# A vision block on one Trainium2 core: the base rows of an image are written one step later in the attention pipeline

## The chip, the cores and the metric

One core of one Trainium2 chip runs the whole kernel. The metric is the device time of one execution in microseconds (us); the figure for a kernel is the median of its runs. The kernel is written engine by engine: TensorE (PE in the profile, its weight loads PEld), VectorE (DVE), ScalarE (ACT), GpSimd (POOL) and SyncE (SP, which issues most DMAs) each run their own in-order program, and semaphores join them.

## The reference

32 images of 256 x 256 go through three stages.

```python
# 1. three-level Haar transform, bands weighted by softmax/sigmoid gates, transformed back
h = _L0_tok_ref(x, Wa, ba, Wd1, bd1, Wd2, bd2, Wd3, bd3)
h = jnp.concatenate([broadcast(cls_tok), h], axis=1)          # 257 tokens of 256
# 2. causal attention of layernorm(h) with itself
e = _layernorm(h)
scores = einsum('bnd,bmd->bnm', einsum('bnd,de->bne', e, R), e) + mask
h = h + einsum('bnm,bmd->bnd', softmax(scores), e)
# 3. eight experts, each takes the k tokens it scores highest
h = h + _L0_ffn_ref(_layernorm(h), gate_w, gamma, beta, fc1s, b1s, fc2s, b2s)
```

The expert stage starts from `xf`, the layernormed rows, and adds the experts' weighted outputs to them, so the result is `h1 + layernorm(h1) + experts`. The attention stage therefore writes two things for every image: the "base rows" `h1 + layernorm(h1)` straight to the output (the scatter of the experts adds to them later), and the "expert rows", the twice-normalised input that the experts gather.

## The kernel before, in words

**Stages.** The images are loaded and their gate logits computed (to about 55 us of the span); then a software pipeline takes the 32 images through transform and attention (55 to 337 us); then 26 bisection rounds find the experts' thresholds (337 to some 400 us); then the experts run to the end.

**The pipeline.** It has 36 steps, one per new image, and 4 more to drain. In step t five images are in flight: image t (called `a`, and `nxt` is t+1), `b` = t-1, `c` = t-2, `d` = t-3 and `m` = t-4. `LAG` is 4. `steps()` (line 259) emits for each engine first `HEAD` steps written out, then a hardware loop (`Fori`, line 267) of four steps per pass (`UNROLL`) up to `TAIL` = 28, then steps 28 to 35 written out. With `HEAD` = 4 the loop makes six passes, steps 4 to 27. An `emit` function per engine fixes that engine's order within a step. In step t:

- TensorE: the inverse transform of `b` into bank `Hb` (L778), four transposes of `c` into `Tb` (L786), the forward transform of `a` (L793), three transposes of the exponentials of `d` (L801), keys of `c` times R (L809), the attention product of `d` (L816 to L818), the scores of `c` into `Sb` (L826, L828).
- VectorE: statistics of `b` from `Hb` (L1140, L1146), the row-sum reciprocal (L1152), band weights and inverse columns of `a` (L1159 to L1177), `U` of `d` from the attention product (L1183), **the update `H1` of `d`** (L1191, two instructions), then gate scores (L1198) and **the negated row maxima of `c`** (L1202), and statistics of `H1` (L1208, L1214).
- GpSimd: waits for the statistics, takes them to the power -0.5 (L475), makes the scales and biases; L480 is the last of them and signals `nrm`. Then it makes the forward columns of image t+1 (L440 to L447; L447 signals `xc`) and stores the statistics (L483).
- ScalarE: **exponentials** of `d` (L598, L600), the copy of the transposed encoding `ET` (L605), the copy of the transposed exponentials `PTS` (L610), **the copy of the inverse** `hc` (L614), the copy of the keys `GT` (L617), the layernormed rows `Ex` of `b` (L624, needs `nrm`), the expert rows `Yp` of `m` (L632) and **the base rows `Bs` of `m`** (L638, two instructions).
- SyncE: stores the base rows of `m` after semaphore `base`, then the expert rows after `yp`.

Two lines tie the base rows to others. Both buffers of `H1` are reused every second image, so VectorE waits before L1191:

```python
after(dve, "base", d.n - 1)        # in step t: base rows of image t-5 are written
```

The exponentials of the next step wait for `nmax` of L1202. `N6`, `O1`, `ST` hold biases, plus-one scales and scales of a step in two buffers by the step's parity.

Of the kernel before, what the change touches and what calls it, by code (L numbers as in the profile page):

```python
# [6 lines left out]
ACT = mybir.ActivationFunctionType  # L7
# [8 lines left out]
NB = 32  # L16
NH = 2
# [30 lines left out]
def build_program(nc, x, cls_tok, Wa, ba, Wd1, bd1, Wd2, bd2, Wd3, bd3, R, gate_w, gate_wT, gamma, beta,  # L48
                  fc1T, b1, fc2T, b2, b2T, const, out, debug=None):
    ctx = ExitStack()  # L50
    with ctx:
        def sb(name, shape, dt=F32):
            return ctx.enter_context(nc.sbuf_tensor(name, shape, dt))

        def sem(name):
            return ctx.enter_context(nc.semaphore(name))
# [121 lines left out]
        H1 = [sb(f"H1{i}", [P, NH, D]) for i in range(2)]  # L178
        Bs = [sb(f"Bs{i}", [P, NH, D]) for i in range(2)]
# [7 lines left out]
        N6 = [sb(f"N6{i}", [P, 6]) for i in range(2)]  # L187
        O1 = [sb(f"O1{i}", [P, 2]) for i in range(2)]
# [43 lines left out]
        s = {n: sem(n) for n in names}  # L232

        def after(eng, name, count):

            if not isinstance(count, int) or count > 0:
                eng.wait_ge(s[name], count)
# [6 lines left out]
        LAG = 4  # L244
# [6 lines left out]
        class Step:  # L251

            def __init__(self, i, k):
                self.n, self.p, self.r = i * UNROLL + k, k % 2, k % 4
                self.h = i * (UNROLL // 2) + k // 2

        HEAD, TAIL = 4, 28

        def steps(eng, emit):


            def images(i, k, bounded):
                return [Step(i, k)] + [Step(i, k + d) if not bounded or 0 <= k + d < NB else None
                                       for d in range(1, -LAG - 1, -1)]
            for k in range(HEAD):
                emit(*images(0, k, True))
            with eng.Fori(HEAD // UNROLL, TAIL // UNROLL) as i:
                for k in range(UNROLL):
                    emit(*images(i, k, False))
            for k in range(TAIL, NB + LAG):  # L270
                emit(*images(0, k, True))
# [295 lines left out]
        def _(act):  # L567
# [5 lines left out]
            A = nc.scalar  # L573
            for h in range(NH):
                for n, levels in enumerate(((1, 3), (2,))):
                    act.wait_ge(s["rep"], 2 * h + n + 1)
                    for lv in levels:
                        last = A.activation(bsum[h][lv], RB[h][lv][1], ACT.Copy)
# [6 lines left out]
            A.activation(z2[:, 1:NJ], z2[:, 1:NJ], ACT.Exp)  # L585
            A.activation(z2[:, 0:1], zz[:, 0:1], ACT.Exp, scale=-1.0).then_inc(s["z_e"], 1)

            def emit(t, _nxt, _a, b, c, d, m):
                if isinstance(t.n, int) and t.n == EARLY + 7:
                    act.wait_ge(s["gt_c"], 6)  # L590
                    A.activation(GM[:, 0:EARLY, :, :], GL[:, 0:EARLY, :, :], ACT.Tanh).then_inc(s["gt_t"], 1)
                if d:

                    after(act, "pt", d.n - 1)
                    after(act, "u", d.n - 1)
                    after(act, "rv", d.n - 1)
                    act.wait_ge(s["nmax"], d.n + 1)
                    A.activation(Pr[d.p][:, 0:129], Sb[:, KEYS[0][0]:KEYS[0][1]], ACT.Exp, bias=nmx[d.p][:, 0:1],  # L598
                                 accum_out=rsm[d.p][:, 0:1])
                    A.activation(Pr[d.p][:, 129:386], Sb[:, KEYS[1][0]:KEYS[1][1]], ACT.Exp, bias=nmx[d.p][:, 1:2],  # L600
                                 accum_out=rsm[d.p][:, 1:2]).then_inc(s["pexp"], 1)
                if c:
                    after(act, "sm", c.n - 1)
                    act.wait_ge(s["et"], c.n + 1)
                    A.activation(ET[c.p][:, :, 1:NT], Tb[:, :].rearrange("p (c t) -> p c t", c=2), ACT.Copy)\  # L605
                        .then_inc(s["et_ev"], 1)
                if d:
                    after(act, "av", d.n - 1)
                    act.wait_ge(s["pt"], d.n + 1)
                    A.activation(PTS[d.p][:, :], Pb[:, 0:384], ACT.Copy).then_inc(s["pt_ev"], 1)  # L610
                if b:
                    after(act, "h1", b.n - 3)
                    act.wait_ge(s["st0_b"], b.n + 1)
                    A.activation(hc[b.r][:, :, :], Hb[:, :].rearrange("p (h c) -> p h c", h=NH), ACT.Copy)  # L614
                if c:
                    act.wait_ge(s["er"], c.n + 1)
                    A.activation(GT[c.p][:, :, NE + 1:], Rb[:, :].rearrange("p (c t) -> p c t", c=2), ACT.Copy)\  # L617
                        .then_inc(s["er_ev"], 1)
                if b:

                    after(act, "av", b.n - 3)
                    act.wait_ge(s["nrm"], t.n + 1)
                    for h in range(NH):
                        last = A.activation(Ex[b.r][:, h, 0:D], Hb[:, h * D:(h + 1) * D], ACT.Identity,  # L624
                                            bias=N6[t.p][:, h:h + 1], scale=ST[t.p][:, 8 + h:9 + h])
                    last.then_inc(s["hcE"], 1)
                if m:

                    after(act, f"yp_st{m.p}", m.h * 16)
                    act.wait_ge(s["nrm"], t.n + 1)  # L630
                    for h in range(NH):
                        last = A.activation(Yp[m.p][:, h, :], H1[m.p][:, h, :], ACT.Identity,  # L632
                                            bias=N6[t.p][:, 4 + h:5 + h], scale=ST[t.p][:, 12 + h:13 + h])
                    last.then_inc(s["yp"], 1)

                    after(act, f"base_st{m.p}", m.h * 16)
                    for h in range(NH):
                        last = A.activation(Bs[m.p][:, h, :], H1[m.p][:, h, :], ACT.Identity,  # L638
                                            bias=N6[t.p][:, 2 + h:3 + h], scale=O1[t.p][:, h:h + 1])
                    last.then_inc(s["base"], 1)  # L640
            steps(act, emit)

            def high(eh, q, layer, half):

                hi = (w1s, w2s)[layer][eh][0]
                act.wait_ge(s["wld"], (q * 2 + layer + 1) * 16)
                A.activation(flat(hi, half), raw[:, half * NF:(half + 1) * NF], ACT.Copy).then_inc(s["whi"], 1)  # L647
# [56 lines left out]
            act.wait_ge(s["ld_par"], 112)  # L704
            high_rows(Job(0, 0))
            jobs(act, emit)


# [811 lines left out]
```

## Time and profile before

| | us |
|---|---|
| median of 3 runs | 878.05 (875.82 to 880.17) |
| the profiled execution's own time | 877.11 |
| its span on the engines | 875.2 |
| the attention pipeline, 36 steps | 282 of it |
| busy share of the span: PE / PEld / DVE | 85% / 72% / 66% |
| busy share of the span: ACT / POOL | 52% / 53% |

The busy shares are averages over stages of different kinds. In the pipeline four engines work in turn on each image, and each is idle part of every step; what sets the pace there is read from who waits for whom.

### The profile page before, as it was taken

To read this page: it belongs to the slowest core of one execution; us is meant where nothing else is said; L and a number is where in the kernel's file an instruction comes from. 1 tells how busy PE (TensorE), PEld (TensorE's weight loads), DVE (VectorE), ACT (ScalarE), POOL (GpSimd) and SP (SyncE) were. 2 spreads that over 40 slices of the span, in tenths; PEclk is the share of its full clock that TensorE was granted. 3 is DMA by queue.
4 is the path that set the end of the run, shared out by engine and by line. 5 is a ranking of instruction groups with operands and counts; after the bars stand their busy time and mean duration, and the time that the engine had idled before them with its cause. 6 is when DMAs were issued, how large, how long until landed. Compare 5 with 4: busy or idle time off the path is not lost.

```text
span 875.2 us, 15546 instructions
## 1 busy us (share of the span) xinstructions
PE 743.0 (85%) x4349; PEld 627.9 (72%) x4349; DVE 580.8 (66%) x1951; ACT 452.6 (52%) x998; POOL 463.5 (53%) x744
## 2 busy tenths in 40 slices
PE   6977999999999972333799897998979989989994
PEld 3644666766676652222698897998979979889994
DVE  3835888888888866988776574574656836544341
ACT  1003677777777763000553765545646655366552
POOL 0127667776777743203336556565475664654723
PEclk9988999999999995555899999998999999989997
DMA  9400121122112226201123233334243342323312
GB/s 347 184 3 1 49 73 54 66 72 72 59 61 72 73 73 108 102 1 44 61 38 95 72 52 87 86 51 128 38 98 79 49 133 43 96 69 51 50 19 31
DMA packets 45448, 64.32 MB, mean 73 GB/s; under 512 B 13840, under 2 KB 40528, under 8 KB 42704
## 3 DMA queue, kind: packets, MB, share of 16 engines
q1 hardware_dynamic: 32400, 46.54, 15.9%
q0 software_dynamic: 12800, 17.12, 12.0%
q8 instruction: 24, 0.39, 0.2%
q14 instruction: 32, 0.26, 0.1%
q10 hardware_dynamic: 192, 0.00, 0.0%
HBM read 38.12 MB, written 25.53 MB: 73 GB/s over the span
## 4 chain that ended last, share of the span: by engine, by line
PE 32%; DVE 8%; issue 8%; POOL 7%; DMA 4%; ACT 3%; POOLq 1%; ACTq 0%; DVEq 0%; SPq 0%
PE bank L885 15%; PE bank L899 12%; DMA raw<-in_fc1T 3%; DVE ge L1242 2%; POOL w2l L494 2%; POOL yg L509 2%; POOL out L531 2%; DVE Tc L1258 1%; PE bank L874 1%; ACT bank L668 1%; PE bank L922 1%; PE bank L864 1%; PE bank L911 1%; DMA yg<-rows,idx 1%; ACT hh L671 1%
## 5 line engine op out<-in xcount | busy, mean ns | idle before, releaser
L1365 DVE TENSOR_TENSOR hl<-bank,hh 128x384 fp32r<-128x384 f32 (+1 forms) x192 | 97.5, 513 | 167.7 <-ACT hh L671 165.4
L531 POOL DMA_INDIRECT out<-ob,sidx x72 | 113.9, 1582 | 165.4 <-ACT ob L684 153.8
L668 ACT ACTIVATE bank<-bank,b1s 128x384 f32<-128x384 f32 (+1 forms) x192 | 99.5, 518 | 134.4 <-PE bank L885 133.9
L885 PE MATMUL bank<-yh,w1h 128*128 128x384 f32 (+1 forms) x384 | 137.8, 359 | 27.4 <-DVE hl L1365 26.1
L885 PE MATMUL bank<-yh,w1l 128*128 128x384 f32 (+1 forms) x384 | 127.5, 332 | 0.0
L885 PE MATMUL bank<-yl,w1h 128*128 128x384 f32 (+1 forms) x384 | 127.4, 332 | 0.0
L899 PE MATMUL bank<-w2l,hh 128*128 128x256 f32 x384 | 108.0, 281 | 0.0
L899 PE MATMUL bank<-w2h,hh 128*128 128x256 f32 x384 | 108.0, 281 | 0.0
L899 PE MATMUL bank<-w2h,hl 128*128 128x256 f32 x384 | 107.9, 281 | 0.0
L509 POOL DMA_INDIRECT yg<-rows,idx x72 | 72.4, 1006 | 62.9 <-issue 57.8
L885 PEld LDWEIGHTS bank<-yh,w1h 128*128 128x128 f32 x384 | 77.3, 201 | 32.7 <-DVE hl L1365 28.7
L671 ACT ACTIVATE hh<-bank 128x384 fp32r<-128x384 f32 (+1 forms) x192 | 87.8, 457 | 6.1
L885 PEld LDWEIGHTS bank<-yl,w1h 128*128 128x128 f32 x384 | 77.0, 200 | 0.0
L885 PEld LDWEIGHTS bank<-yh,w1l 128*128 128x128 f32 x384 | 76.2, 198 | 0.0
L899 PEld LDWEIGHTS bank<-w2l,hh 128*128 128x128 f32 x384 | 72.6, 189 | 0.0
L899 PEld LDWEIGHTS bank<-w2h,hl 128*128 128x128 f32 x384 | 72.5, 189 | 0.0
L899 PEld LDWEIGHTS bank<-w2h,hh 128*128 128x128 f32 x384 | 72.5, 189 | 0.0
L809 PE MATMUL bank<-ET,Rw 128*128 128x256 f32 x256 | 62.9, 388 | 0.0
L494 POOL TENSOR_TENSOR w1l<-raw,w1h 128x1024 fp32r<-128x1024 f32 x16 | 37.8, 2368 | 34.7 <-ACT w1h L647 34.6
L809 PEld LDWEIGHTS bank<-ET,Rw 128*128 128x128 f32 x256 | 45.9, 189 | 11.0 <-issue 5.2
L826 PE MATMUL bank<-GT,ET 128*128 128x137 f32 (+1 forms) x256 | 52.5, 340 | 0.7 <-ACT GT L617 0.7
L475 POOL TENSOR_TENSOR ST<-A,mhalf 128x6 f32<-128x6 f32 x36 | 50.0, 1389 | 3.0
(223 smaller groups left out, 1760.9 us busy)
## 6 DMA issues: line engine op xcount, KB each, us to landing
BIG<-in_x SPq DMA_DIRECT2D x4, 2048.0 KB, 18.9
out<-Bs SPq DMA_DIRECT2D x32, 256.0 KB, 2.2
rows<-Yp SPq DMA_DIRECT2D x32, 256.0 KB, 2.4
raw<-in_fc1T SPq DMA_DIRECT2D x8, 1024.0 KB, 4.8
raw<-in_fc2T SPq DMA_DIRECT2D x8, 1024.0 KB, 4.8
yg<-rows,idx POOLq DMA_INDIRECT x72, 2.9
out<-ob,sidx POOLq DMA_INDIRECT x72, 3.8
gwb<-in_gate_w SPq DMA_DIRECT2D x1, 1024.0 KB, 12.4
```

Of the source, the lines that this page charges most:

```text
L475: g.tensor_tensor(st[:, 8:14], A6[:, :], mhalf[:, :], ALU.pow).then_inc(s["pow"], 1)
L494: rest = g.tensor_tensor(flat(lo, half), raw[:, half * NF:(half + 1) * NF], flat(hi, half), ALU.subtract)
L509: g.indirect_dma_start(out=yg[eh][0:m, t, :], out_offset=None, in_=rows, in_offset=tok(ap=idx[eh][0:m, t:t + 1], axis=0))\
L531: g.indirect_dma_start(out=out_rows, out_offset=tok(ap=sidx[job.eh][0:m, t:t + 1], axis=0), in_=ob[t % 3][0:m, :], in_offset=None, compute ...
L668: A.activation(h[:, 0:cur.w], h[:, 0:cur.w], ACT.Gelu_apprx_tanh, bias=b1s[:, bass.ds(cur.e, 1), f]).then_inc(s["hact"], 1)
L671: A.activation(hT[cur.p][0][:, f, 0:cur.w], h[:, 0:cur.w], ACT.Copy).then_inc(s["hhi"], 1)
L809: last = T.matmul(Rb[:, e * D:(e + 1) * D], Rw[:, j, e * P:(e + 1) * P], ET[c.p][:, j, 1:NT], start=(j == 0), stop=(j == 1))
L826: T.matmul(Sb[:, c0:c0 + w], ET[c.p][:, j, 1 + h * P:1 + (h + 1) * P], GT[c.p][:, j, 0:w], start=(j == 0), stop=False)
L885: last = T.matmul(Lb[ring(cur, f)][:, 0:cur.w], w1s[cur.eh][i][:, d, f * P:(f + 1) * P], yT[cur.p][k][:, d, 0:cur.w], start=(n == 0), stop ...
L899: mm = T.matmul(bank[4 + t % 2][:, 0:D], hT[prev.p][i][:, f, at:at + P], w2s[prev.eh][k][:, f, :], start=(n == 0), stop=(n == 23))
L1242: last = v.tensor_scalar(ge[:, eh, :], V[:, eh, :], tried[:, eh:eh + 1], None, ALU.is_ge, ALU.add, accum_out=cnt[:, eh:eh + 1])
L1365: v.tensor_tensor(hT[cur.p][1][:, f, 0:cur.w], Lb[ring(cur, f)][:, 0:cur.w], hT[cur.p][0][:, f, 0:cur.w], ALU.subtract).then_inc(s["hlo"], 1)
```

## The change

ScalarE's base rows leave the end of step t. A function `base_rows` writes them in step t+1, after the copy of the inverse and ahead of the copy of the keys. In step t it is thus image t-5 whose base rows are written; biases and scales are those of step t-1, found by the image's own parity (the same buffers). The last image's base rows follow after the steps. So that the image five back has a valid index in the first pass of the loop, `HEAD` goes from 4 to 8: on every engine steps 4 to 7 are written out, and the loop makes five passes, steps 8 to 27.

```diff
             def __init__(self, i, k):
                 self.n, self.p, self.r = i * UNROLL + k, k % 2, k % 4
                 self.h = i * (UNROLL // 2) + k // 2
-
-        HEAD, TAIL = 4, 28
+                self.i, self.k = i, k
+
+            def back(self, d):
+
+                return Step(self.i, self.k - d)
+
+        HEAD, TAIL = 8, 28
...
+            def base_rows(m):
+
+                after(act, f"base_st{m.p}", m.h * 16)
+                for h in range(NH):
+                    last = A.activation(Bs[m.p][:, h, :], H1[m.p][:, h, :], ACT.Identity,
+                                        bias=N6[m.p][:, 2 + h:3 + h], scale=O1[m.p][:, h:h + 1])
+                last.then_inc(s["base"], 1)
+
...
                     A.activation(hc[b.r][:, :, :], Hb[:, :].rearrange("p (h c) -> p h c", h=NH), ACT.Copy)
+
+                if not isinstance(t.n, int) or t.n > LAG:
+                    base_rows(t.back(LAG + 1))
                 if c:
                     act.wait_ge(s["er"], c.n + 1)
...
                     last.then_inc(s["yp"], 1)

-                    after(act, f"base_st{m.p}", m.h * 16)
-                    for h in range(NH):
-                        last = A.activation(Bs[m.p][:, h, :], H1[m.p][:, h, :], ACT.Identity,
-                                            bias=N6[t.p][:, 2 + h:3 + h], scale=O1[t.p][:, h:h + 1])
-                    last.then_inc(s["base"], 1)
             steps(act, emit)
+            base_rows(Step(0, NB - 1))
```

ScalarE, one step inside the loop of the kernel before, up to the exponentials of the next step (`Pr` and `Ex` lie in the tile ARENA; L598 and L600 are the exponentials, L632 the expert rows, L638 the base rows):

```order
L614 ACTIVATE hc<-bank 128x512 [waits st0_b,h1]
L617 ACTIVATE GT<-bank 128x2x256 [waits er]
L622 REGISTER_ALU [waits av]
L624 ACTIVATE ARENA<-bank,N,ST 128x256 [waits nrm]
L624 ACTIVATE ARENA<-bank,N,ST 128x256
L632 ACTIVATE Yp<-H,N,ST 128x256 [waits nrm,yp_st1]
L632 ACTIVATE Yp<-H,N,ST 128x256
L638 ACTIVATE Bs<-H,N,O 128x256 [waits base_st1]
L638 ACTIVATE Bs<-H,N,O 128x256
L598 ACTIVATE ARENA,rsm<-bank,nmx 128x129 [waits rv,nmax,u,pt]
```

The same stretch of the changed kernel, where L611 is the first exponential and L597 the base rows:

```order
L627 ACTIVATE hc<-bank 128x512 [waits st0_b,h1]
L597 ACTIVATE Bs<-H,N,O 128x256 [waits base_st0]
L597 ACTIVATE Bs<-H,N,O 128x256
L633 ACTIVATE GT<-bank 128x2x256 [waits er]
L638 REGISTER_ALU [waits av]
L640 ACTIVATE ARENA<-bank,N,ST 128x256 [waits nrm]
L640 ACTIVATE ARENA<-bank,N,ST 128x256
L648 ACTIVATE Yp<-H,N,ST 128x256 [waits nrm,yp_st1]
L648 ACTIVATE Yp<-H,N,ST 128x256
L611 ACTIVATE ARENA,rsm<-bank,nmx 128x129 [waits rv,nmax,u,pt]
```

The two base-row instructions have gone from in front of the exponentials to the place between `hc` and `GT`.

VectorE, the end of step 3 and the begin of step 4, before: the loop is entered there.

```order
L1214 BN_AGGR ST<-bn 128x2 [waits st1_b]
L1214 BN_AGGR ST<-bn 128x2
L267 UNCONDITIONAL_BRANCH
L267 ISA
L1140 BN_STATS bn<-bank 128x6 [waits h0,tab]
L1140 BN_STATS bn<-bank 128x6
L1146 BN_AGGR ST<-bn 128x2 [waits st0_b]
L1146 BN_AGGR ST<-bn 128x2
L1150 REGISTER_ALU
```

The same place in the changed kernel:

```order
L1226 BN_AGGR ST<-bn 128x2 [waits st1_b]
L1226 BN_AGGR ST<-bn 128x2
L1152 BN_STATS bn<-bank 128x6 [waits h0,tab]
L1152 BN_STATS bn<-bank 128x6
L1158 BN_AGGR ST<-bn 128x2 [waits st0_b]
L1158 BN_AGGR ST<-bn 128x2
L1164 RECIPROCAL ST<-rsm 128x2 [waits tab,pexp]
```

Branch and register instructions are gone from steps 4 to 7; the loop is entered four steps later.

## Rows read from the trace of the kernel before

**Rows 1.** Busy time by engine in one pass of the loop; columns as named in its first line.

```profile
core 0: us, PE busy (x) PEld busy (x) DVE busy (x) ACT busy (x) POOL busy (x), PEclk, DMA share, GB/s
125.00:156.70 31.70, 31.15 (x142) 21.59 (x142) 27.42 (x97) 23.50 (x56) 22.89 (x66) 1.00 0.20 66
```

**Rows 2.** Timeline of ScalarE: start, length, engine, line, operation, idle time before.

```profile
126.18 1.08 ACT L632 ACTIVATE Yp<-H,N,ST 128x256 f32<-128x256 f32 x2
127.16 1.08 ACT L638 ACTIVATE Bs<-H,N,O 128x256 f32<-128x256 f32 x2
128.15 0.36 ACT L598 ACTIVATE ARENA<-bank,nmx 128x129 f32<-128x129 f32 x1
...
130.19 0.59 ACT L614 ACTIVATE hc<-bank 128x512 f32<-128x512 f32 x1
131.68 0.60 ACT L617 ACTIVATE GT<-bank 128x512 f32<-128x512 f32 x1 [0.90 <-PE bank L809]
...
135.93 0.37 ACT L598 ACTIVATE ARENA<-bank,nmx 128x129 f32<-128x129 f32 x1
```

**Rows 3.** Timeline of VectorE, steps 8 to 10: update and maxima.

```profile
125.77 1.42 DVE L1191 SCALAR_TENSOR_TENSOR H<-ARENA,ST,hc 128x256 f32<-128x256 f32 x2
...
127.20 0.61 DVE L1202 TENSOR_REDUCE nmx<-bank 128x1 f32<-128x129 f32 x2
...
133.02 0.89 DVE L1183 SCALAR_TENSOR_TENSOR ARENA<-CX,ARENA,bank 128x264 f32<-128x264 f32 x2 [0.68 <-PE bank L818]
134.00 1.20 DVE L1191 SCALAR_TENSOR_TENSOR H<-ARENA,ST,hc 128x256 f32<-128x256 f32 x2
...
135.21 0.61 DVE L1202 TENSOR_REDUCE nmx<-bank 128x1 f32<-128x129 f32 x2
...
141.80 1.04 DVE L1191 SCALAR_TENSOR_TENSOR H<-ARENA,ST,hc 128x256 f32<-128x256 f32 x2
...
142.85 0.61 DVE L1202 TENSOR_REDUCE nmx<-bank 128x1 f32<-128x129 f32 x2
```

**Rows 4.** Timeline of GpSimd, steps 8 to 10: last scale and the columns.

```profile
124.99 0.24 POOL L480 TENSOR_SCALAR O<-ST 128x2 f32<-128x2 f32 x1
...
127.66 0.29 POOL L447 TENSOR_TENSOR ARENA<-ARENA 128x64 f32<-128x64 f32 x1
...
132.64 0.24 POOL L480 TENSOR_SCALAR O<-ST 128x2 f32<-128x2 f32 x1
...
133.98 0.40 POOL L443 TENSOR_TENSOR ARENA<-ARENA 128x128 f32<-128x128 f32 x1
...
140.63 0.24 POOL L480 TENSOR_SCALAR O<-ST 128x2 f32<-128x2 f32 x1
```

**Rows 5.** Timeline of TensorE, step 9: forward transform, transposes, scores.

```profile
128.00 1.13 PE L793 MATMUL bank<-ARENA,C 128*128 128x512 f32 x2
129.19 0.52 PE L801 MATMUL bank<-C,ARENA 128*128 128x128 f32 x3
...
132.82 0.63 PE L826 MATMUL bank<-GT,ET 128*128 128x137 f32 x4
```

**Rows 6.** Timeline of VectorE, first instruction of a later pass of the loop.

```profile
152.70 0.76 DVE L1140 BATCH_NORM_STATS2 bn<-bank 128x6 f32<-128x256 f32 x2 [0.41 <-issue]
```

**Rows 7.** DMA issues of the page: size, us from issue to landing.

```profile
out<-Bs SPq DMA_DIRECT2D x32, 256.0 KB, 2.2
rows<-Yp SPq DMA_DIRECT2D x32, 256.0 KB, 2.4
```

**Rows 8.** Timelines of VectorE and GpSimd in the written-out steps 28 and 29.

```profile
285.35 0.61 DVE L1202 TENSOR_REDUCE nmx<-bank 128x1 f32<-128x129 f32 x2
...
291.00 0.24 POOL L480 TENSOR_SCALAR O<-ST 128x2 f32<-128x2 f32 x1
```

**Rows 9.** Timelines of ScalarE and VectorE, end of step 31 and step 32.

```profile
308.12 1.08 ACT L632 ACTIVATE Yp<-H,N,ST 128x256 f32<-128x256 f32 x2
...
310.09 0.35 ACT L598 ACTIVATE ARENA<-bank,nmx 128x129 f32<-128x129 f32 x1
...
308.82 0.62 DVE L1202 TENSOR_REDUCE nmx<-bank 128x1 f32<-128x129 f32 x2
```

## The prediction

> **What bounds the kernel now.** I read the busy time by stretch first. One pass of the loop, four images, takes 31.7 us, in which TensorE is busy for 31.15, VectorE 27.42, ScalarE 23.50, GpSimd 22.89 [rows 1]. ScalarE has time to spare, so moving its work can pay only through what it holds up. TensorE looks full, but the ends of its matmuls are modelled, so I read waits instead, engine by engine, in the timelines of steps 8 to 10.
>
> On ScalarE base rows run from 127.16 to 128.24, and the exponentials of step 9 start at 128.15, in their wake [rows 2]. The maxima they need were complete at 127.20 + 0.61 = 127.81 [rows 3]. The exponentials were late by 0.34. In step 10 they start at 135.93, and the maxima ended at 135.82: 0.11. The pattern repeats with the loop; summed over the four steps of a pass the lag is 0.34 + 0.12 + 0.34 + 0.33 = 1.13.
>
> A second chain passes ScalarE by. GpSimd's last scale ends at 125.23, 132.88 and 140.87 in steps 8 to 10 [rows 4]; the maxima end at 127.81, 135.82 and 143.46 [rows 3]. From maxima to the next step's last scale it is 132.88 - 127.81 = 5.07 and 140.87 - 135.82 = 5.05. From last scale to maxima it is 2.58, 2.94 and 2.59. Two of three are alike although the update L1191 began 0.54, 1.12 and 0.93 after the scale and lasted 1.42, 1.20 and 1.04. In steps 8 and 10 it ends at 127.19 and 142.84, both times 1.96 or 1.97 after the scale. So a later start is made good by a shorter run: the update is held by GpSimd's column instructions, which run right behind the scale. Starting the update earlier brings nothing there. In step 9 alone it began 0.02 after L443 had started (134.00 against 133.98) and ended 0.36 later than that rule. I take this as the central reading: **in three of four steps the pace comes from VectorE's statistics, GpSimd's scale and the column instructions, and a later exponential costs nothing there.**
>
> **The change, part by part.**
>
> *Base rows ahead of the exponentials, removed.* Expert rows end at 127.26, before the maxima [rows 2, 3], so the exponentials are bound by the maxima and start about 0.04 after them: 0.30 earlier in three steps of four, 0.08 in the fourth, 0.99 per pass.
>
> How much of that reaches the update? The transposes of the exponentials begin at 129.19, 1.04 after them, but TensorE first runs the forward transform, 128.00 to 129.13, which waits for GpSimd's last column at 127.95 [rows 4, 5]. Its end is modelled; between 0.06 (if the end is right) and 0.30 (if it drains early) is to be had. I take 0.2, because its two matmuls show 1.13 together while other groups on TensorE start some 0.1 before a modelled end.
>
> For step 9 the update then starts at about 133.8, some 0.18 before L443, as in step 10, where it starts 0.93 after the scale. It should go ahead of L443, end 1.96 after the scale, and the maxima come at 132.88 + 2.58 = 135.46 instead of 135.82: 0.36 gained. In the other three steps the scale itself follows the maxima before it by an unchanged 5.07, so nothing is gained. Steps of this kind are 5, 9, 13, 17, 21 and 25: 6 x 0.36 = **2.2 us**. Bounds: 0 (the update still loses the turn) and 7 passes x 0.99 = 6.9 (every lead kept).
>
> The Trainium skill, page "SBUF — State Buffer", section "Who interferes with whom", states that a VectorE instruction with two SBUF inputs and a GpSimd one that reads SBUF shut each other out, and that whichever starts first holds the port for its whole length. By that rule a lead of 0.06 would already do for step 9, and the sum would be the same 2.2 with either reading of TensorE; without it the smaller lead gives 0. The updates of steps 8 and 10 [rows 3, 4] agree with the exclusion; no row here has the update start so shortly before a column instruction.
>
> *Base rows between the copy of the inverse and the keys, added.* They take 1.08 together, and 0.98 until the next instruction can start [rows 2]. The gap there is from 130.19 + 0.5 to 131.68, 0.99: ScalarE idles 0.90 of it for TensorE's keys. It fits with nothing over. If it overruns, the scores at 132.82 [rows 5] stand 0.54 behind the end of the keys' copy (132.28), so up to about 0.4 more is covered as well. Cost 0; bounds 0 and, past the cover, 1 to 1 per step. The copy of the inverse keeps its place, and so does `Ex`, which waits for the scale.
>
> *Added wait.* The update of step t now waits for base rows written in the same step. They end about 3.6 after its exponentials; the update starts 5.85 after them (128.15 to 134.00). 2.2 us to spare, cost 0. Were it late, gate scores, maxima and statistics would queue behind it on VectorE.
>
> *The stores.* SyncE issues the base rows' store, then the expert rows' behind it, so both go out about 4 us later than their data now allow. They land in 2.2 and 2.4 us [rows 7], some 7 after the exponentials of that step, and the buffer of the expert rows is written again 5.7 into the next step, that is 13 or 14 after. Cost 0. The last image's base rows follow its expert rows directly, as before, long before the experts gather.
>
> *Steps 4 to 7 written out.* A pass of the loop costs VectorE 0.41 at its first instruction [rows 6]; one such place, at step 8, becomes an entry like that of step 4: at most 0.4 gained. On the other side, in the written-out steps 28 and 29 the scale ends 291.24 - 285.96 = 5.28 after the maxima [rows 8], against 5.07 in the loop: 0.2 lost in about two steps. Together 0; bounds -0.4 and +0.4.
>
> *The end.* From step 31 on GpSimd makes no columns. There expert rows end at 309.20, maxima at 309.44, and the exponentials start at 310.09 [rows 9]. Free of base rows they start 0.04 after maxima that come 0.2 sooner: 309.3, 0.8 gained; step 33 follows its maxima by 0.1 less. The rest drains in series, so **0.9 us** stays; bounds 0.5 and 1.0.
>
> Sum: 2.2 + 0.9 + 0 = 3.1 us. The experts' stage is untouched. The profiled execution took 877.11, 0.94 under the median of 878.05: 874.0 on its terms, 875.0 as a median.
>
> **The rivals.** A difference of 0.5%, 4.4 us, is about what a measurement of this kernel can tell from no change.
>
> *Nothing in the loop.* If the 0.06 is right, the update of step 9 starts at 133.94, 0.04 ahead of L443's recorded start. Whether that is early enough to get the turn no row says. If not, only the end is gained: 878.05 - 0.9 = 877.2. For it: the end of L793 as recorded. Against: matmul ends are modelled.
>
> *Every lead is kept.* If the 1.96 is a coincidence of steps 8 and 10 and the update really follows TensorE (VectorE waits 0.68 for it in step 9), each pass loses 0.99: 6.9 + 0.9 = 7.8, 870.2. For it: that wait, in three steps of four. Against: the sum 1.96 in two different phases, and step 8's update, which took 1.42 where the fastest take less than 1.05.
>
> *Slower: the keys are late.* ScalarE's gap before the keys is exactly filled. If base rows there wait for their store's semaphore, or the copy of the inverse starts later than now, the keys slip, then the scores, then TensorE's next inverse. It decides once the keys start more than 0.4 after their present 3.53 behind the exponentials; a slip of 0.65 would cost 0.25 in each of 28 steps, 7.0 us, of which the end gives back 0.9: 884.2. For it: TensorE shows only 31.70 - 31.15 = 0.55 idle per pass, so it cannot absorb more. Against: the store's buffer was released a step earlier, and nothing ahead of the copy moves back.
>
> **How the numbers follow.** The forecast, a gain of 2 to 4.4 us: 0.52. Nothing in the loop, gain of 0 to 2: 0.21. Every lead kept, or most, over 4.4: 0.20. Slower by over 4.4: 0.07. Faster by over 0.5% is 0.20 and, since single runs before lay between 875.82 and 880.17, 0.07 of the forecast whose median may fall past the bound: 0.27. Slower 0.07; the same is what is left of the forecast, 0.45, and the 0.21: 0.66. The range leaves out the upper end of the slower case and what lies beyond every lead kept: 870.0 to 879.5. The forecast's own range is 873.5 to 876.5.
>
> **What would show it.** Exponentials starting 0.04 behind the maxima in every step; base rows in the gap ahead of the keys, whose start stays 3.5 behind the exponentials; maxima still 2.58 after the last scale, now in step 9 too; a pass of about 31.3 instead of 31.7. It is wrong if a pass is 30.7 or less (the leads are kept), stays 31.7 (the turn is lost), or if the keys move past 3.9.

## The result, and the profile after

The changed kernel takes 873.84 us (median of 18 runs, 870.72 to 876.80) against 877.66 for the kernel before (18 runs, 875.75 to 880.17): ratio 0.9954, 95% interval 0.9942 to 0.9967, a gain of 3.8 us. The forecast was a gain of 3.1. Its profiled execution took 872.07.

The page of the changed kernel, its span and busy times by engine:

```profile
span 870.1 us, 15450 instructions
PE 738.9 (85%) x4349; PEld 627.7 (72%) x4349; DVE 581.5 (67%) x1951; ACT 452.4 (52%) x998; POOL 464.7 (53%) x744
```

Each engine runs as many instructions as before; the 96 that are gone from the total (15546 before) are sequencer instructions. The line numbers move: L611 is the first exponential (L598 before), L597 the base rows (L638), L648 the expert rows (L632), L633 the keys' copy (L617), L1203 the update (L1191), L1214 the maxima (L1202), L485 the last scale (L480), L445 and L446 the two wide column instructions (L440, L441), L448 the first narrow one (L443), L805 the forward transform (L793), L813 the transposes (L801).

To keep out what varies from execution to execution in the rest of the kernel, I measure the pipeline from the end of the maxima of step 3 to the end of those of step 33. The maxima of these two steps on VectorE, in the kernel before:

```profile
87.48 0.60 DVE L1202 TENSOR_REDUCE nmx<-bank 128x1 f32<-128x129 f32 x2
...
324.31 0.61 DVE L1202 TENSOR_REDUCE nmx<-bank 128x1 f32<-128x129 f32 x2
```

and in the changed one:

```profile
88.12 0.61 DVE L1214 TENSOR_REDUCE nmx<-bank 128x1 f32<-128x129 f32 x2
...
321.23 0.61 DVE L1214 TENSOR_REDUCE nmx<-bank 128x1 f32<-128x129 f32 x2
```

That is 236.84 before and 233.12 after: 3.72 us, nearly the whole 3.8 of the medians. A second trace of the changed kernel gives 233.12 again. (The spans differ by 5.1. The rest goes with the execution: the maxima of step 3 came 0.64 later, the last steps took 1.4 less, see the end of this document, and the stages behind 0.6 less.)

ScalarE of the changed kernel, from the expert rows of step 12 to the keys' copy of step 13:

```profile
158.13 1.08 ACT L648 ACTIVATE Yp<-H,N,ST 128x256 f32<-128x256 f32 x2
159.52 0.37 ACT L611 ACTIVATE ARENA<-bank,nmx 128x129 f32<-128x129 f32 x1 [0.31 <-DVE nmx L1214]
161.89 0.59 ACT L627 ACTIVATE hc<-bank 128x512 f32<-128x512 f32 x1
162.37 1.09 ACT L597 ACTIVATE Bs<-H,N,O 128x256 f32<-128x256 f32 x2
163.35 0.60 ACT L633 ACTIVATE GT<-bank 128x512 f32<-128x512 f32 x1
```

The exponentials now wait for the maxima, where they had come in the wake of the base rows [rows 2]; the base rows lie in the gap ahead of the keys. So the change does what it says. VectorE of the changed kernel, update and maxima of step 9, then of steps 12 and 13:

```profile
134.10 1.29 DVE L1203 SCALAR_TENSOR_TENSOR H<-ARENA,ST,hc 128x256 f32<-128x256 f32 x2
135.40 0.61 DVE L1214 TENSOR_REDUCE nmx<-bank 128x1 f32<-128x129 f32 x2
...
157.47 1.32 DVE L1203 SCALAR_TENSOR_TENSOR H<-ARENA,ST,hc 128x256 f32<-128x256 f32 x2
158.80 0.61 DVE L1214 TENSOR_REDUCE nmx<-bank 128x1 f32<-128x129 f32 x2
164.51 0.89 DVE L1195 SCALAR_TENSOR_TENSOR ARENA<-CX,ARENA,bank 128x264 f32<-128x264 f32 x2 [0.56 <-PE bank L830]
165.50 1.02 DVE L1203 SCALAR_TENSOR_TENSOR H<-ARENA,ST,hc 128x256 f32<-128x256 f32 x2
166.53 0.61 DVE L1214 TENSOR_REDUCE nmx<-bank 128x1 f32<-128x129 f32 x2
```

GpSimd of the changed kernel in the same three steps, last scale and columns:

```profile
132.83 0.24 POOL L485 TENSOR_SCALAR O<-ST 128x2 f32<-128x2 f32 x1
...
134.18 0.40 POOL L448 TENSOR_TENSOR ARENA<-ARENA 128x128 f32<-128x128 f32 x1
...
156.94 0.24 POOL L485 TENSOR_SCALAR O<-ST 128x2 f32<-128x2 f32 x1
157.14 0.61 POOL L445 TENSOR_TENSOR ARENA<-BIG 128x256 f32 x1
157.71 0.79 POOL L446 TENSOR_TENSOR ARENA<-BIG 128x256 f32 x1
...
164.23 0.24 POOL L485 TENSOR_SCALAR O<-ST 128x2 f32<-128x2 f32 x1
...
165.57 0.67 POOL L448 TENSOR_TENSOR ARENA<-ARENA 128x128 f32<-128x128 f32 x1
```

From last scale to maxima it was 2.58 to 2.61 in three steps of four and 2.94 in the fourth. It now depends on which instruction goes first at each place, VectorE's update or GpSimd's column instruction ("the turn"):

- **Step 9.** The update started at 134.10, 0.08 ahead of L448, and lost the turn all the same: L448 took its short 0.40, the update 1.29, the maxima came 2.94 after the scale, as before.
- **Step 13.** The update started at 165.50, 0.07 ahead of L448, and won: it took 1.02 and L448 0.67. 2.67 after the scale.
- **Step 12**, the first of a pass. The update started 157.47 - 157.18 = 0.29 after the scale (0.55 before). It now gets in ahead of the second wide column instruction, which starts 0.53 after the scale and takes 0.79 instead of 0.61, and the maxima come 2.23 after the scale instead of 2.58. A pass of the loop takes 30.93 to 31.16 us from step 12 on, where it took 31.65 to 31.68.

Where the 3.72 us come from, by the distance from one step's maxima to the next step's (to 0.02, by the rounding of the rows):

| steps | before | after | gain |
|---|---|---|---|
| 4 to 7 (now written out) | 31.50 | 31.45 | 0.05 |
| 8 | 8.23 | 7.84 | 0.39 |
| 12, 16, 20, 24 (first of a pass) | 32.75 | 31.57 | 1.18 |
| 9, 13, 17, 21, 25 | 40.01 | 39.45 | 0.56 |
| 10, 14, 18, 22, 26 | 38.21 | 38.20 | 0.01 |
| 11, 15, 19, 23, 27 | 39.16 | 38.45 | 0.71 |
| 28 to 31 | 31.50 | 31.20 | 0.30 |
| 32, 33 | 15.48 | 14.96 | 0.52 |

### The profile page after: what moved, and what is told of

Its sections match the earlier page's. It is cut to its first block, busy times and chain, and to the rows that moved or that the text cites. A ratio compares the mean times of both kernels' runs of the same rounds, so it can differ in the third digit from the quotient of the medians.

```text
span 870.1 us, 15450 instructions
## 1 busy us (share of the span) xinstructions
PE 738.9 (85%) x4349; PEld 627.7 (72%) x4349; DVE 581.5 (67%) x1951; ACT 452.4 (52%) x998; POOL 464.7 (53%) x744
## 4 chain that ended last, share of the span: by engine, by line
PE 32%; DVE 8%; issue 8%; POOL 7%; DMA 4%; ACT 3%; POOLq 1%; ACTq 0%; DVEq 0%; SPq 0%
PE bank L897 15%; PE bank L911 12%; DMA raw<-in_fc1T 3%; DVE ge L1254 2%; POOL w2l L499 2%; POOL yg L514 2%; POOL out L536 2%; DVE Tc L1270 1%; PE bank L886 1%; ACT bank L680 1%; PE bank L934 1%; PE bank L876 1%; PE bank L923 1%; DMA yg<-rows,idx 1%; DVE hl L1377 1%
## 5 line engine op out<-in xcount | busy, mean ns | idle before, releaser
L480 POOL TENSOR_TENSOR ST<-A,mhalf 128x6 f32<-128x6 f32 x36 | 50.2, 1394 | 3.0
```

The source lines that it names most:

```text
L480: g.tensor_tensor(st[:, 8:14], A6[:, :], mhalf[:, :], ALU.pow).then_inc(s["pow"], 1)
```

## The experiments

All stage lengths below are from the maxima of step 3 to those of step 33, of one profiled execution each. e3, e5 and e6 leave out part of the work, so their outputs are not the kernel's. The kernels of one group ran on one chip with the kernel before, whose medians there were 878.01 (e1 to e4), 878.69 (e5 to e8) and 877.51 (e9 to e11). A difference of medians between two groups is therefore weaker than the ratio to the kernel before within one.

| run | median | ratio to before, interval | stage |
|---|---|---|---|
| before / changed | 877.66 / 873.84 | 0.9954 (0.9942 to 0.9967) | 236.84 / 233.12 |
| e1 HEAD 8 alone | 878.83 | 1.0008 (0.9994 to 1.0023) | 237.68 |
| e2 end only | 875.69 | 0.9984 (0.9967 to 1.0002) | 236.32 |
| e3 changed, base rows one column wide | 873.36 | 0.9950 (0.9934 to 0.9967) | 232.93 |
| e4 changed, base rows behind the keys | 873.81 | 0.9955 (0.9941 to 0.9970) | 233.41 |
| e5 before, no columns | 874.77 | 0.9957 (0.9940 to 0.9974) | 233.57 |
| e6 changed, no columns | 866.61 | 0.9864 (0.9842 to 0.9886) | 226.30 |
| e7 changed, columns 0.15 later | 874.39 | 0.9962 (0.9941 to 0.9982) | 235.23 |
| e8 changed, HEAD 12 | 872.73 | 0.9931 (0.9910 to 0.9953) | 232.61 |
| e9 changed, wide columns early | 866.41 | 0.9874 (0.9854 to 0.9894) | 227.04 |
| e10 before, wide columns early | 873.96 | 0.9963 (0.9950 to 0.9976) | 233.92 |
| e11 changed, again | 873.20 | 0.9956 (0.9940 to 0.9972) | 233.12 |

### Do GpSimd's columns hold the update? (e5, e6)

The central reading, tried directly, in the kernel before and in the changed one:

```diff
             def columns(m):
...
                 after(po, "z_done", m.n - 1)
+                if not isinstance(m.n, int) or m.n > 1:
+                    apart(po)
+                    g.memset(tick[:, :], 0.0).then_inc(s["xc"], 1)
+                    return
```

> The kernel before without GpSimd's column instructions from image 2 on (an empty instruction signals in their place; the forward transforms read old columns, so the attention is computed of wrong images). Nothing of GpSimd then runs beside VectorE's update. Own theory (GpSimd's columns hold the update): the update never takes more than 1.05 us; base rows ahead of the exponentials now set the pace, a pass takes 30.5 to 31.2 us. Rival (TensorE and the exponentials set the pace anyway): a pass stays within 0.2 us of 31.7.

> The changed kernel without GpSimd's column instructions from image 2 on (as in the run before it). Own theory: with the update free, every lead of the exponentials is kept, and this kernel is 6 us or more faster than the same cut of the kernel before. Rival (the columns have nothing to do with it): the difference between the two stays what it is with columns, about 3.8 us.

The medians are 874.77 and 866.61: deferring the base rows is now worth 8.2 us, against 3.8 with columns. In the stage it is 7.3, and e6's step 33 is slow there for another reason: the granted clock of TensorE was 0.74 from its exponentials to the attention product, which came after 6.57 us instead of 4.89. A pass takes 31.2 us in e5 and 30.0 in e6, 1.2 apart. VectorE of e6, update and maxima of step 13:

```profile
161.38 0.88 DVE L1208 SCALAR_TENSOR_TENSOR H<-ARENA,ST,hc 128x256 f32<-128x256 f32 x2
162.26 0.61 DVE L1219 TENSOR_REDUCE nmx<-bank 128x1 f32<-128x129 f32 x2
```

The update takes 0.88 in all steps of both cuts; beside columns it took 1.02 to 1.42. The columns might also have held it by another way, through the forward transform that waits for them. That is not what changed: in the loop's other steps the update of e6 starts 0.75 to 1.01 after the last scale, in the changed kernel 0.75 to 1.03, and in the first step of a pass it even starts later (step 12: 0.38 against 0.28). What is gained is its length. In e5 the base rows now set the pace. The maxima of its step 12 ended at 157.94; ScalarE of e5 and the update of step 13:

```profile
158.91 0.35 ACT L603 ACTIVATE ARENA<-bank,nmx 128x129 f32<-128x129 f32 x1
...
164.76 0.88 DVE L1196 SCALAR_TENSOR_TENSOR H<-ARENA,ST,hc 128x256 f32<-128x256 f32 x2
165.64 0.61 DVE L1207 TENSOR_REDUCE nmx<-bank 128x1 f32<-128x129 f32 x2
```

The exponentials start 0.97 behind the maxima there, where with columns the lag had been 0.34. So the columns hold the update, and with them gone the base rows ahead of the exponentials cost time. The rival that the difference stays 3.8 falls.

### Is it the place of the columns, or their work? (e7, e9, e10)

e7 moves one small copy in front of the columns of the changed kernel:

```diff
+                g.tensor_copy(TST[:, bass.ds(t.n, 1), :].rearrange("p b k -> p (b k)"), st[:, :]).then_inc(s["tab"], 1)
                 if nxt:
                     columns(nxt)
-                g.tensor_copy(TST[:, bass.ds(t.n, 1), :].rearrange("p b k -> p (b k)"), st[:, :]).then_inc(s["tab"], 1)
```

> The changed kernel with GpSimd's copy of the statistics (0.19 us) ahead of the column instructions, which start some 0.15 us later after the last scale. Own theory (the update ends where the columns let it): in the steps behind a return of the loop (9, 21, 25), where the update began just behind L443's counterpart and ended 0.36 us late, it now goes first: maxima 2.6 to 2.75 us after the scale instead of 2.94; in the others they come up to 0.15 later. Net within 2 us of the changed kernel. Rival (the forward transform's end sets the exponentials' transposes, and the columns its start): 0.15 us per step, 4 us slower than the changed kernel.

GpSimd of e7 in step 13, last scale and first wide column instruction:

```profile
163.70 0.24 POOL L485 TENSOR_SCALAR O<-ST 128x2 f32<-128x2 f32 x1
164.05 0.60 POOL L445 TENSOR_TENSOR ARENA<-BIG 128x256 f32 x1
```

VectorE of e7 in steps 13 and 14:

```profile
164.97 1.08 DVE L1203 SCALAR_TENSOR_TENSOR H<-ARENA,ST,hc 128x256 f32<-128x256 f32 x2
166.05 0.61 DVE L1214 TENSOR_REDUCE nmx<-bank 128x1 f32<-128x129 f32 x2
...
172.65 1.18 DVE L1203 SCALAR_TENSOR_TENSOR H<-ARENA,ST,hc 128x256 f32<-128x256 f32 x2
173.84 0.61 DVE L1214 TENSOR_REDUCE nmx<-bank 128x1 f32<-128x129 f32 x2
```

From scale to maxima it is 2.71 to 2.73 in every step of the loop but the first of a pass: 0.15 more than 2.58, the whole shift of the columns. In steps 9, 13, 17, 21 and 25 the update always gets its turn. So the columns pin the maxima in place. The stage is 2.1 us longer than the changed kernel's, just over the 2 that I allowed and half of what the rival wanted. The medians don't show it: e7 is 4.3 us under the kernel before on its chip (interval of the ratio 0.9941 to 0.9982), the changed kernel 3.8.

e9 and e10 split the columns instead. The two wide ones, which need no statistics, go to where GpSimd waits for VectorE (in the changed kernel and in the one before):

```diff
+                if nxt:
+                    wide_columns(nxt)
                 if b:
                     after(po, "hcE", b.n - 1)
                     po.wait_ge(s["st0"], b.n + 1)
...
                 if nxt:
-                    columns(nxt)
+                    narrow_columns(nxt)
```

> The changed kernel with GpSimd's two wide column instructions (1.2 us, they need no statistics) moved from behind the last scale to the 1.6 us in which it waits for VectorE's next statistics; behind the scale only the four narrow ones are left. Own theory (the update is held by the wide columns, the transposes by the forward transform that waits for the last column): last scale to maxima falls from 2.58 to 2.3 to 2.45 in every step, a pass from 31.1 to 30.0 to 30.5, the time to about 869. Rival (what is gained is lost again at the statistics, since the columns then delay the scale): a pass within 0.2 us of the changed kernel's.

> The kernel before with the same move of GpSimd's wide columns; base rows stay ahead of the exponentials. Own theory: now the base rows set the pace, a pass takes about 31.2 us as in the cut without columns, and deferring the base rows (the run before this one) is worth 5 us or more instead of 3.8. Rival: the worth of deferring them stays 3.8 us.

GpSimd of e9 in step 13: the first statistics instruction, the last scale, and behind it the first narrow column instruction; then a wide one of the next image:

```profile
157.79 0.23 POOL L481 TENSOR_SCALAR A<-ST 128x4 f32<-128x4 f32 x1 [0.80 <-DVE ST L1165]
...
160.47 0.24 POOL L491 TENSOR_SCALAR O<-ST 128x2 f32<-128x2 f32 x1
160.67 0.40 POOL L452 TENSOR_TENSOR ARENA<-ARENA 128x128 f32<-128x128 f32 x1
...
163.38 0.61 POOL L444 TENSOR_TENSOR ARENA<-BIG 128x256 f32 x1
```

VectorE of e9 in step 13:

```profile
161.62 0.99 DVE L1210 SCALAR_TENSOR_TENSOR H<-ARENA,ST,hc 128x256 f32<-128x256 f32 x2
162.61 0.61 DVE L1221 TENSOR_REDUCE nmx<-bank 128x1 f32<-128x129 f32 x2
```

Still 0.80 idle ahead of the statistics, so the scale is not delayed; scale to maxima 2.51 (a little over the 2.3 to 2.45 expected; 2.04 in the first step of a pass); a pass of 30.4. The time is 866.41, 11.1 under the kernel before and 6.8 under the changed one on the same chip (873.20, e11), for an order of instructions alone. e10 has the same split without deferred base rows: 873.96, a pass of 31.2. Deferring them is worth 7.6 us there. The rival (worth stays 3.8) falls a second time, here in kernels that leave nothing out.

### Steps written out, and the end (e1, e8, e2)

```diff
-        HEAD, TAIL = 4, 28
+        HEAD, TAIL = 8, 28
```

> The kernel before with only HEAD from 4 to 8: base rows stay ahead of the exponentials. Own theory (the written-out steps cost what the loop's steps cost, and one return of the loop at step 8 is saved): the maxima of step 7 come within 0.1 us of where they are before relative to those of step 3 (31.5 us), those of step 8 some 0.35 us sooner after them, nothing else changes; time 0.4 us under before. Rival (the written-out steps carry the gain of the change): 2 us or more under before.

Neither came. The stage is 0.84 us longer, 237.68, the median 0.8 higher with an interval that spans no change. Step 8 keeps 8.21, and passes take 31.77 to 31.94 instead of 31.66. VectorE of e1, update and maxima of step 12:

```profile
158.67 1.23 DVE L1191 SCALAR_TENSOR_TENSOR H<-ARENA,ST,hc 128x256 f32<-128x256 f32 x2
159.92 0.61 DVE L1202 TENSOR_REDUCE nmx<-bank 128x1 f32<-128x129 f32 x2
```

ScalarE of e1, base rows of step 12 and the exponentials behind them:

```profile
160.17 1.08 ACT L638 ACTIVATE Bs<-H,N,O 128x256 f32<-128x256 f32 x2
161.15 0.35 ACT L598 ACTIVATE ARENA<-bank,nmx 128x129 f32<-128x129 f32 x1
```

In step 12 the maxima end at 160.53, 2.30 after the scale: the update has got in ahead of the wide column instruction, as in the changed kernel. The scale came 5.73 after the maxima here (5.62 before), and the update starts 0.44 after it, 0.09 ahead of that instruction. But the base rows are in front of the exponentials, which start 0.62 later than the maxima allow (0.34 before), and the next step gives all back and more (8.26 for step 13, 8.00 before). So the early turn in a pass's first step is of use only with the base rows out of the way, as in the changed kernel, where it makes the 1.18. And the written-out steps by themselves bring nothing. No run defers the base rows all through the loop with `HEAD` at 4, so how much of the 1.18 needs the written-out steps is not shown.

e8 takes `HEAD` to 12 in the changed kernel.

> The changed kernel with HEAD 12 instead of 8: steps 8 to 11 written out too, one return of the loop less. Own theory (as for HEAD 8 alone): 0 to 0.6 us faster than the changed kernel. Rival (written-out steps are better for the phase of update and columns): 1.5 us or more faster.

Stage 0.51 shorter than the changed kernel's, within my 0 to 0.6. Steps 13, 17, 21 and 25 all win their turn here (2.65 or 2.66), two more than in the changed kernel, worth 0.27 each: that alone is about the 0.51. The medians can't tell the two theories apart. e8 is 6.0 us under the kernel before on its chip, the changed kernel 3.8, and the intervals of the ratios overlap; it is the stage that speaks against the rival's 1.5.

e2 is the kernel before with only the base rows of images 27 to 31 deferred (`HEAD` stays 4):

```diff
+                if late_base(t, 32):
+                    base_rows(t.back(LAG + 1))
                 if c:
                     act.wait_ge(s["er"], c.n + 1)
...
+                    if not late_base(t, 31):
+                        base_rows(m)
```

> The kernel before, base rows deferred only from step 31 on (images 27 to 31), HEAD stays 4. Own theory: exponentials of step 32 start 0.04 us after the maxima of step 31 instead of 0.65, those of step 33 about 0.1 us closer to their maxima; the maxima of step 33 come 0.8 to 0.9 us sooner, the time falls by 0.9 us, steps up to 31 as before. Rival (the end drains in series with something else): under 0.3 us.

Steps up to 31 are as before, steps 32 and 33 take 14.96 instead of 15.48: 0.52, not 0.8 to 0.9. Step 31 can't gain here, since the base rows of step 30 still run ahead of its exponentials. In step 32 the exponentials now start 0.12 after the maxima instead of 0.65, and in step 33 they had started 0.12 after them already. The interval of the ratio, 0.9967 to 1.0002, holds both. The end of the changed kernel, exponentials of step 32 and the maxima of step 31 they follow:

```profile
307.00 0.37 ACT L611 ACTIVATE ARENA<-bank,nmx 128x129 f32<-128x129 f32 x1 [0.43 <-DVE nmx L1214]
...
306.27 0.61 DVE L1214 TENSOR_REDUCE nmx<-bank 128x1 f32<-128x129 f32 x2
```

### Do base rows cost anything in their new place? (e3, e4)

```diff
+                w = D if isinstance(m.n, int) and m.n < 2 else 1
                 for h in range(NH):
-                    last = A.activation(Bs[m.p][:, h, :], H1[m.p][:, h, :], ACT.Identity,
+                    last = A.activation(Bs[m.p][:, h, 0:w], H1[m.p][:, h, 0:w], ACT.Identity,
```

> The changed kernel, but from image 2 on the two base-row instructions write one column of 256 each; the stores go on as they are, so the output's base rows are not computed for those images. Own theory (base rows in their new place are hidden behind TensorE's keys): maxima of steps 8 to 31 within 0.1 us per pass of four of the changed kernel's, time the same within 1 us. Rival (they delay the keys, the scores or the layernormed rows): 0.1 us or more per step faster, 3 us or more in all.

ScalarE of e3, base rows and keys' copy of step 13:

```profile
161.54 0.66 ACT L598 ACTIVATE Bs<-H,N,O 128x1 f32<-128x1 f32 x2
162.35 0.60 ACT L634 ACTIVATE GT<-bank 128x512 f32<-128x512 f32 x1
```

Base rows take 0.66 instead of 1.09, and stage (232.93 against 233.12) and median (873.36) stay; the 0.19 is less than the 0.27 of the one more turn that is won here (steps 9, 17 and 25). The keys do feel them: in step 13 they start 3.66 after the exponentials here and 3.83 in the changed kernel, in step 12 it is 3.55 and 3.72. That slip costs nothing: the base rows are hidden.

e4 emits `base_rows` after the keys' copy instead of ahead of it.

> The changed kernel with the base rows one place later, behind the copy of the keys instead of ahead of it. ScalarE idles 0.6 to 1.2 us there for the scale, and base rows take 0.98, so the layernormed rows start up to 0.35 us late in three of four steps. Own theory (the pace is set past ScalarE, by maxima to scale and scale to update): the layernormed rows have little to spare against TensorE's next inverse; 0 to 2 us slower than the changed kernel. Rival (TensorE's order sets the pace, any delay of its next inverse counts in full): 0.2 us per step, 5 us or more slower than the changed kernel.

Stage 0.3 us longer, the median the same (873.81). The 0.3 is one turn less: the update wins in step 25 alone. In step 13 the layernormed rows start 0.19 after the scale instead of 0.03, and nothing follows: the maxima come 2.94 after the scale, as in every lost turn. So the base rows are covered on the other side of the keys too.

### Is the turn a matter of chance? (e11)

> The changed kernel once more, unchanged, for a second trace. Own theory (the update of a step behind a return of the loop starts so near L443's counterpart that the turn falls either way): maxima 2.66 or 2.94 us after the scale in steps 9, 13, 17, 21, 25, in another mixture than before, all other steps as before to 0.05 us. Rival (each step has its fixed place): the same mixture, 2.94 in 9, 21, 25 and 2.66 in 13, 17.

In the second trace the update wins in steps 17 and 21 (2.65, 2.66 from scale to maxima) and loses in 9, 13 and 25 (2.93); in the first it won in 13 and 17. VectorE in step 9 and step 13 of the second trace:

```profile
133.64 1.29 DVE L1203 SCALAR_TENSOR_TENSOR H<-ARENA,ST,hc 128x256 f32<-128x256 f32 x2
...
165.03 1.29 DVE L1203 SCALAR_TENSOR_TENSOR H<-ARENA,ST,hc 128x256 f32<-128x256 f32 x2
```

All other steps agree with the first trace to 0.02. So a step's place is not fixed. It isn't a plain toss either. In the five traces of the changed kernel, e3, e4, e8 and e11, 24 steps have the update start 0.069 to 0.085 ahead of the narrow column instruction. It won in all 9 with a lead of 0.077 or more, lost in all 6 with 0.073 or less, and in the 9 between them it won 3. What varies from one execution to the next is a few nanoseconds, and they decide over 0.27 us each time.

## Why the prediction was right, point by point

- **Base rows ahead of the exponentials, removed: right in kind.** The exponentials follow the maxima in every step, by 0.11 and not 0.04; only in the first step of a pass by 0.03. The lag of 1.13 per pass fell to some 0.4, so the lead was 0.7 and not 0.99 (the lags I had read give 0.97).
- **"How much of that reaches the update": the 0.2 was too large.** The update of steps 9 and 13 starts 1.03 after the scale instead of 1.12, a lead of 0.09. TensorE of the changed kernel in step 13 shows why: the forward transform, then the transposes, which the exponentials could have allowed at 160.56 (1.04 after 159.52):

```profile
159.95 1.13 PE L805 MATMUL bank<-ARENA,C 128*128 128x512 f32 x2
160.92 0.49 PE L813 MATMUL bank<-C,ARENA 128*128 128x128 f32 x3
```

The wait for the last column isn't all of it: in e6, without columns, the transposes of step 13 still start 1.38 after the exponentials (1.40 here), behind TensorE's own earlier work.

- **"6 x 0.36 = 2.2 us": the term was mis-sized.** The steps of this kind inside the loop gained 0.56. With 0.09 of lead the update starts 0.07 ahead of L448, just where the turn falls either way; it is won in two steps of five, and then 0.28 is saved and not 0.36. In step 5, now written out, the distance fell from 8.01 to 7.86, and step 6 gave back more (7.65 to 7.86).
- **"In the other three steps nothing is gained": true of one of the three, and the other two made up for the loss.** The first step of a pass gained 0.26 to 0.32 each, 1.18 in all. I had taken the end of the update, 1.96 after the scale, as a fixed pin. It holds only while the update starts later than the wide column instruction; at 0.29 after the scale it goes ahead. I asked who goes first for step 9 alone. The trace of the kernel before had the same question in step 8, where the second wide column instruction starts 0.01 ahead of the update's 125.77 [rows 3]:

```profile
125.76 0.61 POOL L441 TENSOR_TENSOR ARENA<-BIG 128x256 f32 x1
```

A lead of 0.2, as I had reckoned with, takes the update past it. The last step of each pass gained 0.02 in step 11 and 0.16 to 0.18 in the later ones, because its scale came 5.07 to 5.09 after the maxima instead of 5.22 to 5.25. The time is on GpSimd: the power of -0.5 starts 3.01 or 3.02 after the maxima in step 15 of both kernels, and the biases behind it at 4.53 instead of 4.68. Deferred base rows are not the reason, since e1 has 5.07 to 5.09 in these steps too; beyond that the cause is open.
- **Steps 4 to 7 and the entry at step 8: 0.05 and 0.39**, within the bounds of -0.4 and 0.4. But e1 shows that the 0.39 belongs to the deferred base rows: with `HEAD` alone step 8 keeps 8.21.
- **The end: 0.9 forecast, 0.82 found.** I had the maxima of step 31 come 0.2 sooner, 0.6 from the lag in step 32, and 0.1 in step 33. Step 31 gained 0.26, step 32 0.52 (the lag fell from 0.65 to 0.12), step 33 nothing.
- **Base rows ahead of the keys, the added wait, the stores: 0, as forecast.** The keys start 3.55 behind the exponentials in two steps of four (3.53 to 3.56 before), 3.65 to 3.72 in the first step of a pass and 3.84 in steps 9, 13, 17, 21 and 25. Up to 0.17 of that is the base rows' (e3), and it stays within the 0.4 that I took to be covered.
- **The rivals.** "Every lead is kept" would need the columns out of the way: once they are, deferring the base rows is worth 8.2 us (e5, e6) or 7.6 (e9, e10), about its 7.8. "Nothing in the loop" came true in steps 9, 21 and 25, three of the five it was about. "The keys are late" fell: the keys stay under 3.9, and e3, with hardly any base rows, isn't faster.

Sum: 0.05 + 0.39 + 1.18 + 0.56 + 0.01 + 0.71 + 0.82 = 3.72. The mechanism of the central reading stands: GpSimd's columns hold the update. Its conclusion, that three steps of four gain nothing, does not. That the loop came out near the forecast is luck: two errors nearly cancelled, 2.2 us forecast from steps that gave 0.56, and nothing from steps that gave 1.90. The end is where sum and mechanism agree. A pass came out at 30.93 to 31.16, between the 31.3 forecast and the 30.7 that would have spoken for every lead kept.

## What to carry to other kernels

Before removing a wait in a pipeline, look for a second chain that reaches the same instruction: here the exponentials moved up by 0.2 to 0.3 us in three steps of four, and little of it reached the maxima until GpSimd's columns moved. A constant distance from another engine's instruction at different starting phases is the sign of being held, and it ends where the start passes that of the instruction before: ask who goes first in every step, not in one. The cure is to move what holds. Here that was worth 6.8 us more (866.41 against 873.20) where the change had brought 4.3 on the same chip, and the change itself was then worth 7.6.

## What the runs showed of the hardware that was not expected

- **The turn between VectorE and GpSimd isn't settled by the recorded starts when they are near.** In the changed kernel's first trace the update started 0.07 to 0.08 ahead of L448 in five steps and won in two (L448 0.67, update 1.02) and lost in three (0.40 and 1.29). Over five traces the border lies at a lead of 0.073 to 0.077 by recorded starts, and with more than that it always won. The Trainium skill's rule, "SBUF — State Buffer", section "Who interferes with whom", is that the one that issues first holds the port and the other blocks. The traces agree in kind (both lengths trade places); the lead of 0.06 in recorded starts that I took from it as enough is not.
- **A held instruction shows as a longer one, on either engine**: the update took 0.88 alone, 1.02 to 1.42 beside the columns, the wide column instruction 0.61 or 0.79.
- **The last steps depend on TensorE's granted clock, which differs between executions.** The attention product of step 34 falls where TensorE has little to do. In the kernel before, the granted clock from the exponentials at 325.03 to the use of the product at 330.36 was 0.70 (1.00 up to 327, 0.50 from 328 on), and the stretch took 5.33:

```profile
325.03:330.36 5.33, 3.50 (x9) 2.16 (x9) 2.63 (x9) 1.73 (x6) 3.76 (x9) 0.70 0.29 100
```

In the changed kernel's first trace the same stretch of work took 3.92 at the full clock, in its second (e11) 4.63 at 0.83:

```profile
321.96:325.88 3.92, 2.09 (x9) 1.37 (x9) 2.62 (x8) 2.38 (x7) 2.66 (x4) 1.00 0.00 0
...
321.50:326.13 4.63, 2.80 (x9) 1.65 (x9) 2.63 (x8) 2.38 (x7) 3.22 (x6) 0.83 0.12 40
```

All thirteen traces fit that: 3.92 at 1.00 (also e2, e7, e8, e10), 5.32 or 5.33 at 0.68 to 0.71 (also e1, e4, e9), the others between. From the maxima of step 33 to the last scale it took 11.74 before and 10.30 after, but 10.31 in e2 and 11.73 in e4. The 1.4 us go with the execution, not with the change.
